# Counting stage of a four-layer graph network: one wait per visit, written-out strips, one load of four bounds, four slots, and 48 scatters moved

## What is computed

```python
def _gin_conv(x, src, dst, W1, b1, W2, b2):
    agg = jax.ops.segment_sum(x[src], dst, num_segments=N_NODES)
    h = x + agg
    h = jnp.maximum(h @ W1 + b1, 0.0)
    return h @ W2 + b2
...
x = _layernorm(x + _L0_gnn_ref(...))   # two gin_conv
x = _layernorm(x + _L1_gnn_ref(...))   # two attention convolutions
x = _layernorm(x + _L2_gnn_ref(...))   # four recurrent (GRU) blocks
x = _layernorm(x + _L3_gnn_ref(...))   # messages along edges
```

## Time and profile before

| what | us |
|---|---|
| median of 3 runs (lowest, highest) | 5777.11 (5770.11, 5782.44) |
| the profiled execution | 5773.72 |
| its span in the profile | 5772.1 |
| counting stage, from PE's first visit to ACT's last copy | 148 to 879 |
| GRU stage, from PE's first product to the next stage's first transfer | 4104 to 4645 |

### The profile page before, as it was taken

The page is one execution under the profiler, slowest core; times in us unless marked ns, Lnnn a source line. Parts: engine busy times, 40 slices in busy tenths (PEclk is TensorE's granted clock), DMA queues, the critical chain, the costliest instruction groups (busy, mean ns, idle before and its releaser), DMA issues. The chain is left out here.

```text
span 5772.1 us, 99298 instructions
## 1 busy us (share of the span) xinstructions
PE 4128.6 (72%) x26079; PEld 2946.9 (51%) x26080; DVE 3743.2 (65%) x9069; ACT 1302.6 (23%) x3162; POOL 3482.7 (60%) x3600
## 2 busy tenths in 40 slices
PE   3777768893577787786365666665899958877886
PEld 2333335562465666664255555564455546655664
DVE  8777772454698898898366666666655445555555
ACT  0111111203232232233211111111344322222222
POOL 2222224553677777773277777773477767777774
PEclk7899999996698899898677777777899978899887
DMA  6000005212444444443433232333322232222334
GB/s 247 13 17 17 16 14 203 72 40 66 125 121 129 122 121 130 122 120 87 149 77 84 76 83 76 84 76 100 108 57 56 67 91 78 78 78 78 78 79 59
DMA packets 331209, 503.85 MB, mean 87 GB/s; under 512 B 104981, under 2 KB 245679, under 8 KB 321030
## 3 DMA queue, kind: packets, MB, share of 16 engines
q0 software_dynamic: 126224, 272.11, 18.3%
q1 hardware_dynamic: 203398, 226.18, 12.6%
q10 hardware_dynamic: 1392, 3.47, 0.2%
HBM read 402.70 MB, written 98.78 MB: 87 GB/s over the span
## 5 line engine op out<-in xcount | busy, mean ns | idle before, releaser
L1146 POOL DMA_INDIRECT e_ring<-att_rows,e_near x1760 | 1778.2, 1010 | 550.7 <-issue 484.7
L1217 PE MATMUL e_psum<-e_ring,e_whole_pick 128*128 128x264 f32 (+1 forms) x3520 | 838.1, 391 | 209.0 <-DVE e_ring L1392 158.7
L2161 POOL DMA_INDIRECT e_nodes<-x,e_edges x832 | 807.6, 971 | 267.6 <-issue 230.1
L1217 PEld LDWEIGHTS e_psum<-e_ring,e_whole_pick 128*128 128x128 f32 x3520 | 640.9, 226 | 333.6 <-issue 163.4
L1170 PE MATMUL e_px<-t_parts,e_pick 128*128 x5280 | 677.0, 269 | 91.1 <-DVE e_prod L1306 40.1
L1306 DVE TENSOR_TENSOR e_prod<-e_px,e_ring 128x512 f32<-128x512 f32 x660 | 450.4, 683 | 434.0 <-DMA e_ring<-att_rows,e_near 328.8
L1652 POOL DMA_INDIRECT sorted<-r_held,r_slot x404 | 394.9, 978 | 277.1 <-DMA r_held<-in_edge_rows 151.7
L321 PE MATMUL b_acc<-b_pick_key,b_pick_lo 128*128 x1960 | 467.8, 366 | 113.5 <-DVE b_pick_key L280 111.5
L1170 PEld LDWEIGHTS e_px<-t_parts,e_pick 128*128 128x128 bf16 x5280 | 444.3, 107 | 178.7 <-issue 108.9
L1260 ACT ACTIVATE e_whole_pick<-e_pturn 128x512 f32<-128x512 bf16 x440 | 261.8, 595 | 1159.3 <-PE e_pturn L1206 1130.5
L1296 DVE TENSOR_REDUCE e_dots<-e_prod 128x8 f32<-128x512 f32 (+1 forms) x660 | 445.3, 675 | 0.0
(11 more groups left out here) (389 smaller groups left out, 7038.8 us busy)
## 6 DMA issues: line engine op xcount, KB each, us to landing
e_relb<-place SPq DMA_DIRECT2D x56, 1024.0 KB, 6.1
e_ring<-att_rows,e_near POOLq DMA_INDIRECT x1760, 2.6
sorted<-o_fill SPq DMA_DIRECT2D x11, 2508.0 KB
e_edges<-sorted SPq DMA_DIRECT2D x209, 132.0 KB
kept<-gin_counts SPq DMA_DIRECT2D x5, 4000.0 KB, 35.0
r_held<-in_edge_rows SPq DMA_DIRECT2D x202, 66.0 KB, 2.1
e_nodes<-x,e_edges POOLq DMA_INDIRECT x832
gru_late<-kept SPq DMA_DIRECT2D x3, 4000.0 KB, 32.5
```

The costliest lines, as they stand in the source:

```text
L1146: pool.indirect_dma_start(out=ring[:, s, r, 0:wd + HEADS], out_offset=None, in_=xrows, in_offset=bass.IndirectOffsetOnAxis(ap=near[:, s, r ...
L1217: mm = pe.matmul(psum[q % 2][:, 0:RING], whole_pick[:, q % 2, c, :], ring[:, s, q * G + c, :], start=(c == 0), stop=(c == G - 1))
L2161: pool.indirect_dma_start(out=nodes[:, q, u, :], out_offset=None, in_=source, in_offset=bass.IndirectOffsetOnAxis(ap=edges[:, q, u, RBF + ...
```

## The change

- Constants stage: the bounds are stored plus one and three places further on, so that a tile's four bounds stand together (`AHEAD = 3`).
- PE: the tile loop is written out, all 25 tiles, so that addresses and most waited-for values are constants. A tile's four window ends come by one load of four values. The beginning of a window is the end of the one before. Visits are numbered from 1.
- PE waits for `picked` once per visit and counts `used` up once per visit. DVE does the same on its side.
- Four slots (`HELD`) hold the one-hot matrices. The room comes from laying the stage's inputs (`dst`, `src`, `hit`) over them; they are read before the first one-hot is written.
- 9 scatters per tile instead of 7 (24 x 9 = 216 instead of 168), and 356 in the GRU stage instead of 404.

```diff
+HELD = 4
+AHEAD = 3
...
-                dve.tensor_copy(K["bounds"][:, :], row[:, :])
+                dve.tensor_scalar(K["bounds"][:, AHEAD:], row[:, :], 1.0, None, ALU.add)
...
-        dst = m.sb("b_dst", [P, LASTS, STEP], I32)
-        src = m.sb("b_src", [P, LASTS, STEP], I32)
+        pick_key = m.sb("b_pick_key", [P, HELD, 2, KEYS], BF16)
+        area = pick_key[:, :, :, :].rearrange("p s b c -> p (s b c)")
+        dst, src, hit = (area[:, i * LASTS * STEP * 2:(i + 1) * LASTS * STEP * 2].bitcast(dt).rearrange("p (k e) -> p k e", k=LASTS)
+                         for i, dt in enumerate((I32, I32, F32)))
...
-        pick_lo = m.sb("b_pick_lo", [P, 2, 2, P], BF16)
-        pick_key = m.sb("b_pick_key", [P, 2, 2, KEYS], BF16)
+        pick_lo = m.sb("b_pick_lo", [P, HELD, 2, P], BF16)
...
                 for n in range(VISITS):
+                    s = (n + 1) % HELD
+                    if n >= HELD:
+                        dve.wait_ge(used, n - HELD + 1)
                     for b in range(2):
-                        if n >= 2:
-                            dve.wait_ge(used, n * 2 + b - 3)
...
+                    key.then_inc(picked, 1)
...
-                with pe.Fori(0, NT) as t:
-                    edges = [pe.value_load(K["bounds"][0:1, ds(t * PER + q, 1)], min_val=min(q, 1), max_val=VISITS)
-                             for q in range(PER + 1)]
-                    for q in range(PER):
-                        pe.wait_ge(moved, t * (2 * PER) + q * 2 + 2)
+                begin = 1
+                for t in range(NT):
+                    _, ends = nc.values_load_multi_w_load_instructions(
+                        K["bounds"][0:1, AHEAD + t * PER + 1:AHEAD + t * PER + 1 + PER], engines=(mybir.EngineType.PE,),
+                        min_val=2, max_val=VISITS + 1)
+                    for q, end in enumerate(ends):
+                        pe.wait_ge(moved, (t * PER + q) * 2 + 2)
...
-                        with pe.Fori(edges[q], edges[q + 1]) as n:
-                            pair = pe.snap(n & 1)
+                        with pe.Fori(begin, end) as n:
+                            s = pe.snap(n & (HELD - 1))
+                            pe.wait_ge(picked, n)
                             for b in range(2):
-                                pe.wait_ge(picked, n * 2 + b + 1)
                                 for h, a, z in halves:
...
-                                mm.then_inc(used, 1)
+                            mm.then_inc(used, 1)
...
+                        begin = end
...
-COUNT_SENDS = (0, 7, NT - 1)
+COUNT_SENDS = (0, 9, NT - 1)
...
-SENT = 404
+SENT = 356
```

More of the change, by code:

```diff
@@ L176, in build_counts @@
         m = Mem(nc, ctx)
-        dst = m.sb("b_dst", [P, LASTS, STEP], I32)
-        src = m.sb("b_src", [P, LASTS, STEP], I32)
+        pick_key = m.sb("b_pick_key", [P, HELD, 2, KEYS], BF16)
+        area = pick_key[:, :, :, :].rearrange("p s b c -> p (s b c)")
+        dst, src, hit = (area[:, i * LASTS * STEP * 2:(i + 1) * LASTS * STEP * 2].bitcast(dt).rearrange("p (k e) -> p k e", k=LASTS)
+                         for i, dt in enumerate((I32, I32, F32)))
         lof = m.sb("b_lof", [P, LASTS, STEP])
         keyf = m.sb("b_keyf", [P, LASTS, STEP])
-        hit = m.sb("b_hit", [P, LASTS, 2 * P])
         bits = hit[:, :, :].bitcast(I32)
@@ L275, in _ @@
                 for n in range(VISITS):
+                    s = (n + 1) % HELD
+                    if n >= HELD:
+                        dve.wait_ge(used, n - HELD + 1)
                     for b in range(2):
-                        if n >= 2:
-                            dve.wait_ge(used, n * 2 + b - 3)
-                        dve.tensor_scalar(pick_lo[:, n % 2, b, :], lane[:, 0:P], lov[:, b, n:n + 1], None, ALU.is_equal)
-                        dve.tensor_scalar(pick_key[:, n % 2, b, :], lane[:, :], keyv[:, b, n:n + 1], None,
-                                          ALU.is_equal).then_inc(picked, 1)
+                        dve.tensor_scalar(pick_lo[:, s, b, :], lane[:, 0:P], lov[:, b, n:n + 1], None, ALU.is_equal)
+                        key = dve.tensor_scalar(pick_key[:, s, b, :], lane[:, :], keyv[:, b, n:n + 1], None, ALU.is_equal)
+                    key.then_inc(picked, 1)
             @block.scalar
@@ L315, in _ @@
                                       start=True, stop=False, skip_group_check=True)
-                        with pe.Fori(edges[q], edges[q + 1]) as n:
-                            pair = pe.snap(n & 1)
+                        with pe.Fori(begin, end) as n:
+                            s = pe.snap(n & (HELD - 1))
+                            pe.wait_ge(picked, n)
                             for b in range(2):
-                                pe.wait_ge(picked, n * 2 + b + 1)
                                 for h, a, z in halves:
                                     mm = pe.matmul(acc[q % 2][:, h, 0:z - a],
-                                                   pick_lo[:, ds(pair, 1), b, :].rearrange("p o c -> p (o c)"),
-                                                   pick_key[:, ds(pair, 1), b, a:z].rearrange("p o c -> p (o c)"),
+                                                   pick_lo[:, ds(s, 1), b, :].rearrange("p o c -> p (o c)"),
+                                                   pick_key[:, ds(s, 1), b, a:z].rearrange("p o c -> p (o c)"),
                                                    start=False, stop=False, skip_group_check=True)
-                                mm.then_inc(used, 1)
+                            mm.then_inc(used, 1)
                         for h, a, z in halves:
@@ L1863 @@
 ROWW = RBF + 2
-COUNT_SENDS = (0, 7, NT - 1)
-GIN_SENDS = [(7 * (NT - 1), 15, 6), (7 * (NT - 1) + 90, 2, 44)]
-TABLE_SENDS = (7 * (NT - 1) + 178, 16, 2)
-GRU_SENDS = 7 * (NT - 1) + 210
+COUNT_SENDS = (0, 9, NT - 1)
+GIN_SENDS = [(9 * (NT - 1), 15, 6), (9 * (NT - 1) + 90, 2, 44)]
+TABLE_SENDS = (9 * (NT - 1) + 178, 16, 2)
+GRU_SENDS = 9 * (NT - 1) + 210
 SEND = 2
-SENT = 404
+SENT = 356
 NSC = GRU_SENDS + SENT
@@ L2422, in gnn_program @@
         K = dict(identf=m.sb("identf", [P, P]), identb=m.sb("identb", [P, P], BF16),
-                 bounds=m.sb("bounds", [1, NWIN + 1], I32))
+                 bounds=m.sb("bounds", [1, AHEAD + NWIN + 1], I32))
         last = m.sb("steps", [P, NT + 2])
```

## The result

The changed kernel takes 5625.25 us (median of 4 runs, 5618.73 to 5629.78) against 5773.61 (4 runs): ratio 0.9743, 95% interval 0.9732 to 0.9755. The forecast was 5657; its range, 5608 to 5700, held the result. In the prediction's own measure, from PE's first visit to ACT's last copy, the stage is now 599 us long where 624 were forecast. A second profile of the changed kernel has a counting stage of 630.8 us, so tenths of a microsecond there mean nothing.

A forecast was written before the change was run, and what follows sets the result against it. PE's register instructions and branch were taken to bound the counting stage. Savings of 66 (waits), 50 (load, loop) and 13 (GRU end), less 9 (clock), made 120 us off 5773.7; with 3.4 us to the median, 5657, range 5608 to 5700.

The forecast's parts named there:

- One wait per visit: Counting stage, PE: fewer register operations between a visit's halves, at window openings and loop heads save 66 us (20 to 110).
- Four slots worth nothing: Counting stage: four slots gain nothing in a steady stretch; they would matter if PE fell under 1.00 us a visit.
- One load of four, loop written out: Counting stage, tile changes: PE's pause falls from 4.11 to 2.1 us at 25 tiles, saving 50 us (33 to 61).
- The clock: Counting stage: PE's clock at half after tile changes costs 18 us if at every tile; half taken, 9 us lost.
- Scatters: Two more per tile in the counting stage cost nothing; 48 fewer in the GRU stage save 13 us (6 to 19).
- DVE's wait for PE "larger in total": Counting stage, a sign of being right: DVE would wait for PE longer in total than the 177.8 us before.
- the fetching case: PE's written-out code stalls on instruction fetches: at every back branch, some 6280 us, chance 0.02; at borders only, 5695, chance 0.10.
- not half: Rival, counting stage: PE's clock stays at half throughout, total 5794 us, slower; chance 0.02.
- PE gains more: Rival: register operations at upper ends, cheap load of four, clock holds: 5593 us, half way 5625; chance 0.14.

The follow-up runs named there:

- the load alone: Kernel before with the tile loop written out and one load of four bounds per tile, two waits and two slots kept: 5694.1 us, ratio 0.9853.
- the single wait alone: Kernel before with one wait and one release per visit on PE and DVE, two slots and five loads kept: 5759.83 us, ratio 0.997.

## Why the prediction was right, and where it missed

**The bound** was read rightly: PE's register instructions set the pace, and the wait "for DVE" in front of PE's products named a bystander, as the leads show. More DVE work in the changed kernel cost nothing; less work on PE's sequencer paid each time, though with two slots only in part.

**One wait per visit** (66 us): the size was right, the account was not. Of the 66, some 8 belong to the window openings, and the run with the load alone shows them with the written-out loop. The other 58 stand against 684.6 - 631.1 = 53.5, or 0.11 us a visit; but only 38.4 of it came without the four slots.

**Four slots worth nothing** was the wrong step. I argued from a steady stretch and left out the 25 pauses, behind which a kernel with one release per visit needs the lead. They are worth 15 us in the changed kernel and 31 with the old pauses; without them the single wait alone gained 17.

**One load of four, loop written out** (50 us) gave 80 by itself, 65 of it at the tile changes. The four checks came at the forecast 1.16 us. Mis-sized was the load, 0.82 with its hop where it is 0.39: I took the middle of the bounds, and the lower one, "no cheaper than one, 0.36", was nearly the value. The 0.15 us of rest were not there either. The Trainium skill's figure of some 200 ns per register even in bulk (Runtime: NRT & Kernel Launch, Instruction fetch mechanics), by which I had reckoned a sum 4 us higher, does not hold for this load: three values more took 0.035 us. There the Trainium skill reckons with it the loads in a launch's preamble; these bounds are read from the core's own memory (SBUF), so I had carried the figure over to another case.

**The clock** (9 us lost) cost next to nothing. It fell at 4 of 23 tile changes, not at half; and the price was wrong as well, since with four slots a fall at 20 of them left the visits as long.

**Scatters:** two more per tile cost nothing, as forecast. The 48 fewer were worth 16 and not 13, because 4.24 us pass from the last store's issue (4487.95) to the next stage, where I took the middle of 0 and 12.5, and DVE's last normalisation ended 1.0 us earlier in the stage. That 24 would have done was not said. The last scatter's instruction ended 52 us before the last store's issue, where I said near 60.

**DVE's wait for PE "larger in total"** was wrong: 44 us.

The rivals: eleven packets came where I expected about ten, and the longest step behind a back branch excludes a stall of 1.6 us for any of them, so neither form of the fetching case happened. The Trainium skill's block size (same page and section) fits the number of packets; its rule that a taken branch out of the current blocks waits for a fetch is neither borne out nor excluded, for no run here shows such a wait. The clock's mean is 0.98, not half. "PE gains more" was nearest in time, 5625 half way to it, by two of its three conditions: the cheap load and the clock that holds.

Term by term in the counting stage: 22 us more from the load and the loop (with the window openings), 9 from the clock, 5 less from waits and slots, so 133 in place of 107.

## What to carry to other kernels

Where one engine's register instructions set the pace, count instructions per step and not their durations alone (here each cost some 0.05 us besides its own): one load of several values, one wait, one fused clamp. Whether the wait that a view names is real, the lead tells: how long its product had been ready. When waits are made coarser, give the producer more slots in the same edit, and judge slots by the stretch behind the longest pause, since in a steady stretch they look worthless. When work is moved off an end, work out the point at which the next thing is last: here half of the move was enough.

## What the hardware showed that I had not expected

- A register load of four 32-bit values takes 0.332 us, of one 0.297; of four 16-bit values 0.987. What makes the 16-bit load dear was not tried.
- With four slots PE's clock fell behind a pause of 2.4 us at 20 of 23 tile changes, behind 1.38 us at 4, behind 0.52 us at none, and the visits within windows took 447.4, 447.6 and 446.7 us in all. The pause alone does not decide: the version with the load alone fell at 10 of 23 behind 1.35 us.
- DVE at 590 of 597 us busy lengthened nothing: a full engine is not the bound while slots let it work through the other's pauses.
